# Three layer normalisations taken into the batch loops, and an edge gather that comes before its projection

## The chip, the cores and the metric

The kernel runs on one core of a Trainium2 chip, in float32 but for one stage. The metric is the device time of one launch, in microseconds.

## The reference, cut to what matters

`x` is 16 batches of 512 rows and 128 features, `adj` a 512 x 512 matrix. Four graph layers follow each other, each as `x = layernorm(x + layer(x))` over the 128 features of a row: (0) eight Euler steps, (1) attention over all nodes, (2) a filter in the eigenbasis of the graph's Laplacian, (3) attention along 256 edges `src -> dst`. The diff touches the normalisations behind layers 1, 2 and 3 and the first half of layer 3:

```python
def _layernorm(x, axis=-1, eps=1e-05):
    m = jnp.mean(x, axis=axis, keepdims=True)
    v = jnp.var(x, axis=axis, keepdims=True)
    return (x - m) / jnp.sqrt(v + eps)
# layer 2, U the eigenvectors
agg = jnp.einsum('mn,bnd->bmd', U.T, features)
h = jax.nn.relu(agg @ W1 + b1)
return jnp.einsum('nm,bmd->bnd', U, h @ W2 + b2)
# layer 3, 4 heads
Xq = (H @ W_lin.T).reshape(bt, n, h, dh)
Xv = (H @ W_val.T).reshape(bt, n, h, dh)
Qs, Kt = Xq[:, src], Xq[:, dst]
e = jnp.einsum('behd,hd->beh', jax.nn.leaky_relu(Qs + Kt, LRELU_SLOPE), a)
e = e + jnp.log(A0[src, dst] + EPS)[None, :, None]
# softmax over the edges of one src, then
Y = jax.ops.segment_sum(attn[..., None] * Xv[:, dst], src, num_segments=n)
return Y @ W_out.T
```

## The kernel before, in words

The program is a row of stages, each a block in which every engine has its own list of instructions and waits on semaphores; a stage begins when all engines have left the one before. The Laplacian, its tridiagonal form, its eigenvectors and layer 0 take the first 3390 us or so; then come `attend` (layer 1), `filter_spectrum` (layer 2) and `edge_attend` (layer 3). The whole of `x` stays in SBUF as `m.x`, 128 partitions x 16 batches x 4 chunks x 128 features.

`Norm` normalises all 16 batches at once. VectorE takes the statistics of 64 chunks (L1356), forms mean and variance of all rows in seven small operations (L1358 to L1364), ScalarE takes the square root (L1379), VectorE the reciprocal, and then both scale the chunks, VectorE 40 (L1369) and ScalarE 24 (L1382). It stands behind the batch loops of `attend`, `filter_spectrum` and `edge_attend`, and once ahead of `attend`.

`filter_spectrum` runs over the batches. ScalarE copies a batch into `xs` (`stage`, L1618). TensorE's turn b is: `aggregate` of batch b+1 (L1584), the hidden layer of b (L1601), `spread` of b-1 (L1592), the output `op` of b (L1607). VectorE adds the bias into `o` when `op` is ready (L1646) and then adds `spread`'s result to `x` (L1641, `finish`).

`edge_attend` has a set-up on VectorE (L1835 to L1850: one-hot matrices of `src` and `dst`), a product that picks rows of `adj` (`picked`, L1720), and then two loops over the batches. Loop A: GpSimd copies a batch into `xs` (L1698, L1701), TensorE transposes it (L1727), projects it to queries and values (L1734) and gathers the rows of both ends by one-hots, with 16 matmuls of 128 columns (L1746, L1749); ScalarE moves the results in between (L1803, L1808); VectorE takes two copies from PSUM and forms the scores (L1862 to L1868). Softmax over edges follows for all batches at once. Loop B: VectorE weights the values into `msg` (L1894), TensorE scatters them (L1787) and projects them (L1780) with a copy by ScalarE in between (L1826), VectorE adds the result to `x` (L1904, `finish`). VectorE's order is message b, then `finish` of b-1; TensorE's is scatter b, then projection of b-1. After the last `Norm`, SP issues 16 stores (L1709).

The loops are `batches(...)`: two batches written out, then a loop instruction over pairs, then the last ones written out. A matmul in float32 shows as two passes in the trace, so that "x8" is four matmuls.

Of the kernel before, what the change touches and what calls it, by code (L numbers as in the profile page):

```python
# [1403 lines left out]
def attend(nc, m):  # L1404


    with ExitStack() as ctx:
# [63 lines left out]
        def _(act):  # L1471
# [28 lines left out]
            norm.scalar(act)  # L1500

        @block.vector
        def _(dve):
# [56 lines left out]
            norm.vector(dve)  # L1560


def filter_spectrum(nc, m):

    with ExitStack() as ctx:  # L1565
        (staged, agg_ready, agg_taken, hid_ready, hid_taken, o_ready, o_taken, y_ready, y_taken) = sems(
            nc, ctx, "f_staged f_agg_ready f_agg_taken f_hid_ready f_hid_taken f_o_ready f_o_taken f_y_ready f_y_taken")
        sb = lambda n, *s: ctx.enter_context(nc.sbuf_tensor("f_" + n, [P, *s], F32))
        xs, agg, hid, o = sb("xs", 2, C, F), sb("agg", 2, N), sb("hid", N), sb("o", 2, C, F)
# [4 lines left out]
        norm = Norm(nc, ctx, m, "f_norm")  # L1574
        block = ctx.enter_context(nc.Block())
        whole = lambda b: m.x[:, b] if isinstance(b, int) else m.x[:, bass.ds(b, 1), :, :].rearrange("p o c f -> p (o c) f")

        @block.tensor
        def _(pe):
            def aggregate(b, u):  # L1580
                pe.wait_ge(staged, b + 1)
                after(pe, agg_taken, b - 1)
                for c in range(C):
                    t = nc.tensor.matmul(aggp[:, u, :], xs[:, u, c, :], m.U[:, c, :], start=(c == 0), stop=(c == C - 1))  # L1584
                t.then_inc(agg_ready, 1)

            def spread(b, u):
                pe.wait_ge(o_taken, b + 1)
                after(pe, y_taken, b - 1)
                for r in range(C):  # L1590
                    for c in range(C):
                        t = nc.tensor.matmul(yp[:, u, r, :], m.UT[:, c, r * P:(r + 1) * P], o[:, u, c, :], start=(c == 0),  # L1592
                                             stop=(c == C - 1))
                t.then_inc(y_ready, 1)

            def batch(b, u):
                if not isinstance(b, int) or b < B - 1:
                    aggregate(b + 1, 1 - u)
                pe.wait_ge(agg_taken, b + 1)
                after(pe, hid_taken, b)  # L1600
                nc.tensor.matmul(hidp[:], m.w["L2_gnn_W1"][:], agg[:, u, :], start=True, stop=True).then_inc(hid_ready, 1)  # L1601
                if not isinstance(b, int) or b > 0:
                    spread(b - 1, 1 - u)
# [5 lines left out]

            aggregate(0, 0)  # L1610
            batches(pe, batch, B - 1)
            spread(B - 1, (B - 1) % 2)

        @block.scalar
        def _(act):
            def stage(b, u):
                after(act, agg_ready, b - 1)
                nc.scalar.activation(xs[:, u], whole(b), ACT.Copy).then_inc(staged, 1)  # L1618

            def batch(b, u):  # L1620
                if not isinstance(b, int) or b < B - 1:
                    stage(b + 1, 1 - u)
                act.wait_ge(agg_ready, b + 1)
                after(act, hid_ready, b - 1)
                nc.scalar.activation(agg[:, u, :], aggp[:, u, :], ACT.Copy).then_inc(agg_taken, 1)
# [3 lines left out]

            stage(0, 0)  # L1630
            batches(act, batch, B - 1)
            norm.scalar(act)

        @block.vector
        def _(dve):
# [3 lines left out]
            def finish(b, u):  # L1639
                dve.wait_ge(y_ready, b + 1)  # L1640
                v.tensor_tensor(whole(b), whole(b), yp[:, u], ALU.add).then_inc(y_taken, 1)  # L1641

            def batch(b, u):
# [3 lines left out]
                if not isinstance(b, int) or b > 0:  # L1647
                    finish(b - 1, 1 - u)

            batches(dve, batch, B - 1)  # L1650
            finish(B - 1, (B - 1) % 2)
            dve.wait_ge(y_taken, B)
            norm.vector(dve)
# [8 lines left out]
def edge_attend(nc, m, out):  # L1662

    with ExitStack() as ctx:
        (step, prep, prep_taken, picked, log_go, log_done, ready, staged, xT_ready, xT_taken, qv_ready, qv_taken, gath_ready,
         gath_taken, eT_ready, eT_taken, erow_ready, erow_taken, exp_go, exp_done, den_ready, msg_ready, yT_ready,
         yT_taken, y_ready, y_taken, stored) = sems(
            nc, ctx, "e_step e_prep e_prep_taken e_picked e_log_go e_log_done e_ready e_staged e_xT_ready e_xT_taken e_qv_ready "
                     "e_qv_taken e_gath_ready e_gath_taken e_eT_ready e_eT_taken e_erow_ready e_erow_taken e_exp_go "
                     "e_exp_done e_den_ready e_msg_ready e_yT_ready e_yT_taken e_y_ready e_y_taken e_stored")  # L1670
        sb = lambda n, *s: ctx.enter_context(nc.sbuf_tensor("e_" + n, [P, *s], F32))
        src_of, dst_of, both = sb("src_of", C, E), sb("dst_of", C, E), sb("both", C, E)
# [4 lines left out]
        loga, xs, xT = sb("loga", Q), sb("xs", C, F), sb("xT", N)  # L1677
        qv = sb("qv", 2, C, 2 * F)
# [17 lines left out]
        @block.gpsimd  # L1696
        def _(pool):
            nc.gpsimd.tensor_copy(xs[:], m.x[:, 0]).then_inc(staged, 1)  # L1698
            with pool.Fori(1, B) as b:
                pool.wait_ge(xT_ready, b)  # L1700
                nc.gpsimd.tensor_copy(xs[:], m.x[:, bass.ds(b, 1), :, :].rearrange("p o c f -> p (o c) f")).then_inc(staged, 1)  # L1701

        @block.sync
        def _(sp):
            sp.wait_ge(norm.dve_part, 1)
# [7 lines left out]
        def _(pe):  # L1713
# [10 lines left out]
            def transpose(b):  # L1724
                pe.wait_ge(staged, b + 1)
                for c in range(C):
                    t = nc.tensor.transpose(tp[:, c, :], xs[:, c, :], m.ident[:])  # L1727
                t.then_inc(xT_ready, 1)

            def project(b):  # L1730
                pe.wait_ge(xT_taken, b + 1)
                after(pe, qv_taken, b)
                for c in range(C):
                    t = nc.tensor.matmul(qvp[:, c, :], xT[:, c * P:(c + 1) * P], wqv[:], start=True, stop=True)  # L1734
                t.then_inc(qv_ready, 1)

            def gather(b, u):
                if not isinstance(b, int) or b < B - 1:
                    project(b + 1)
                if not isinstance(b, int) or b < B - 2:  # L1740
                    transpose(b + 2)
                pe.wait_ge(qv_taken, b + 1)
                after(pe, gath_taken, b)
                for q in range(Q):
                    for c in range(C):
                        nc.tensor.matmul(gp[:, q, 0:F], both[:, c, q * P:(q + 1) * P], qv[:, u, c, 0:F], start=(c == 0),  # L1746
                                         stop=(c == C - 1))
# [48 lines left out]
        def _(act):  # L1796
# [3 lines left out]
            def take_xT(b):  # L1800
                act.wait_ge(xT_ready, b + 1)
                after(act, qv_ready, b)
                nc.scalar.activation(xT[:].rearrange("p (c n) -> p c n", c=C), tp[:], ACT.Copy).then_inc(xT_taken, 1)  # L1803

            def take_qv(b, u):
# [189 lines left out]
```

## Time and profile before

| | us |
|---|---|
| three runs | 4143.9, 4145.84, 4145.85; median 4145.84 |
| profiled execution | 4153.18 |
| its span, first to last instruction | 4151.4 |
| from the last sum of layer 1 to the end of the span | 492 |

Over the span TensorE is busy for 69%, VectorE for 76%, ScalarE for 21%, GpSimd for 29%; TensorE's granted clock is 0.65 of full speed in the mean. These shares are those of the long first part; each stage behind it has its own. "Granted clock" is 0.5 (1.2 GHz) or 1.0 (2.4 GHz) at any time, and what lies between is a mean over a stretch. In the timeline a row is a run of equal instructions: its start, its length, engine, line, operation, output and inputs, count, and in brackets the idle time ahead of it and who ended that. The end of a matmul is modelled and lies somewhat behind the start of what follows it.

### The profile page before, as it was taken

To read this page: it belongs to the slowest core of one execution; us is meant where nothing else is said; L and a number is where in the kernel's file an instruction comes from. 1 tells how busy PE (TensorE), PEld (TensorE's weight loads), DVE (VectorE), ACT (ScalarE), POOL (GpSimd) and SP (SyncE) were. 2 spreads that over 40 slices of the span, in tenths; PEclk is the share of its full clock that TensorE was granted. 3 is DMA by queue.
4 is the path that set the end of the run, shared out by engine and by line. 5 is a ranking of instruction groups with operands and counts; after the bars stand their busy time and mean duration, and the time that the engine had idled before them with its cause. 6 is when DMAs were issued, how large, how long until landed. Compare 5 with 4: busy or idle time off the path is not lost. (4 is left out here: it accounts for less than half of the span.)

```text
span 4151.4 us, 77402 instructions
## 1 busy us (share of the span) xinstructions
PE 2843.8 (69%) x21043; PEld 2136.5 (51%) x21043; DVE 3157.0 (76%) x18105; ACT 864.7 (21%) x3720; POOL 1218.4 (29%) x5211
## 2 busy tenths in 40 slices
PE   4778778777776666665558667748496446769694
PEld 3666666666654545444448434425353225646662
DVE  4888888888888888888873788899999548942463
ACT  1212222222223333333320001001010002321201
POOL 1554555555555555555550111000000000000000
PEclk8555555555555555555555778879798668889868
DMA  1000000000000000000011000000000000000001
GB/s 59 2 2 2 2 2 2 2 2 2 2 2 2 1 2 1 1 1 1 1 55 32 1 1 1 1 1 0 0 1 0 0 0 0 0 0 0 0 1 41
DMA packets 23019, 23.83 MB, mean 6 GB/s; under 512 B 3024, under 2 KB 21328, under 8 KB 22096
## 3 DMA queue, kind: packets, MB, share of 16 engines
q1 hardware_dynamic: 22608, 19.17, 1.4%
q8 instruction: 158, 2.59, 0.3%
q14 instruction: 253, 2.07, 0.2%
HBM read 14.97 MB, written 4.19 MB: 5 GB/s over the span
## 5 line engine op out<-in xcount | busy, mean ns | idle before, releaser
L373 PE MATMUL h_sums<-h_P,ones 128*128 128x60 f32 (+3 forms) x1020 | 315.3, 404 | 244.3 <-DVE h_P L559 165.8
L831 PE MATMUL d_acc<-d_h,U 128*128 128x512 f32 x1024 | 471.4, 604 | 0.0
L381 PE MATMUL h_axp<-h_XV,ident 128*128 128x64 f32 x1018 | 337.2, 435 | 184.4 <-POOL h_XV L425 184.4
L354 PE MATMUL h_sums<-h_parts,ones 128*128 128x19 f32 (+2 forms) x1020 | 315.5, 399 | 188.0 <-DVE h_parts L512 163.0
L373 PEld LDWEIGHTS h_sums<-h_P,ones 128*128 128x128 f32 x1020 | 255.0, 310 | 304.9 <-issue 304.9
L362 PE MATMUL h_axp<-h_XV,x 128*128 128x4 bf16 x11514 | 388.5, 169 | 17.0 <-DVE h_CX L523 16.5
L354 PEld LDWEIGHTS h_sums<-h_parts,ones 128*128 128x128 f32 x1020 | 256.7, 312 | 273.9 <-DVE h_parts L512 234.1
L381 PEld LDWEIGHTS h_axp<-h_XV,ident 128*128 128x128 f32 x1018 | 254.4, 310 | 267.4 <-DVE h_y L597 218.3
L411 POOL TENSOR_TENSOR h_root<-urow,h_halves 128x1 f32<-128x1 f32 x510 | 278.1, 545 | 380.2 <-DVE urow L564 380.2
L362 PEld LDWEIGHTS h_axp<-h_XV,x 128*128 128x128 bf16 x11514 | 362.6, 105 | 33.9 <-DVE h_CX L523 25.4
L831 PEld LDWEIGHTS d_acc<-d_h,U 128*128 128x128 f32 x1024 | 188.8, 195 | 202.2 <-issue 202.2
L432 ACT ACTIVATE h_ntau<-h_EE 128x1 f32<-128x1 f32 x510 | 101.5, 199 | 845.9 <-DVE h_EE L595 835.3
L472 ACT ACTIVATE h_XV<-h_XV,urow 128x1 f32<-128x1 f32 x382 | 133.7, 382 | 567.0 <-DVE urow L577 567.0
L882 POOL TENSOR_TENSOR m_c_mid<-m_c_m,m_halves 128x4 f32<-128x4 f32 x53 | 53.4, 1008 | 545.1 <-DVE m_c_m L1135 545.1
L1105 DVE RECIPROCAL m_work<-m_work 128x512 f32<-128x512 f32 (+8 forms) x53 | 206.3, 3892 | 0.0
L844 ACT ACTIVATE d_h<-d_acc 128x512 f32<-128x512 f32 x128 | 76.5, 598 | 535.7 <-PE d_acc L831 524.6
L821 PEld LDWEIGHTS d_acc<-G,d_xT 128*128 128x128 f32 x1152 | 156.4, 201 | 59.6 <-issue 55.5
L1698 POOL COPY e_xs<-x 128x512 f32<-128x512 f32 x1 | 0.6, 611 | 630.0 <-POOLq L1565 630.0
L564 DVE COPY urow<-h_sums 128x2 f32<-128x2 f32 x510 | 80.8, 159 | 125.4 <-PE h_sums L354 123.9
L401 POOL TENSOR_TENSOR h_XV<-h_XV 128x4 f32<-128x4 f32 (+3 forms) x510 | 101.0, 198 | 227.3 <-DVE h_XV L621 183.3
L600 DVE SCALAR_TENSOR_TENSOR h_zp<-h_y,h_EE,below 128x4 f32<-128x4 f32 (+3 forms) x510 | 125.7, 247 | 53.5 <-DVE h_y L597 0.5
L821 PE MATMUL d_acc<-G,d_xT 128*128 128x128 f32 x1152 | 158.7, 286 | 3.1 <-ACT d_xT L844 3.1
(566 smaller groups left out, 6975.9 us busy)
## 6 DMA issues: line engine op xcount, KB each, us to landing
cut<-in_c_cut SPq DMA_DIRECT2D x1, 4608.0 KB, 14.0
x<-in_x SPq DMA_DIRECT2D x16, 256.0 KB, 4.3
out<-x SPq DMA_DIRECT2D x16, 256.0 KB, 3.6
adj<-in_adj SPq DMA_DIRECT2D x1, 1024.0 KB, 5.2
below<-in_c_below SPq DMA_DIRECT2D x1, 1024.0 KB, 7.3
neps<-in_c_neps SPq DMA_DIRECT2D x1, 1024.0 KB, 8.4
UT<-in_c_ramp SPq DMA_DIRECT2D x1, 1024.0 KB, 10.3
same<-in_c_same SPq DMA_DIRECT2D x1, 448.0 KB, 9.9
```

Of the source, the lines that this page charges most:

```text
L354: nc.tensor.matmul(PS1[:, lo:hi], m.ones[:], parts[:, lo:hi], start=True, stop=True).then_inc(sums_ready, 1)
L362: t = nc.tensor.matmul(AX4[:, r, :], part[:, c, r * P:(r + 1) * P], XVb[:, c, 2 * XS + 1::68], start=(c == c0 and i == 0), stop=(c == C - ...
L373: nc.tensor.matmul(PS2[:, :, T1 * c0:], m.ones[:], P2[:, :, c0:, :].rearrange("p i c t -> p i (c t)"), start=True, stop=True).then_inc(pv_ ...
L381: nc.tensor.matmul(sides(PSE), m.ident[:, r:r + 1].broadcast_to([P, P]), sides(XV[:, cr, 0:2 * RIGHT]), start=True, stop=True).then_inc(ro ...
L401: do(g.tensor_tensor(XV[:, c0:, RS], XV[:, c0:, XS], XVb[:, c0:, 2 * XS + 1], ALU.subtract))
L411: g.tensor_tensor(root[:], TT[:, k, 4:5], halves[:], ALU.pow).then_inc(root_done, 1)
L432: copy = lambda out, in_, **k: nc.scalar.activation(out, in_, ACT.Copy, **k)
L472: t = nc.scalar.activation(XV[:, c, vslot(k):vslot(k) + 1], XV[:, c, ES:ES + 1], ACT.Identity, scale=TT[:, k, 3:4], bias=XV[:, c, XS:XS + 1])
L600: zp_done = do.send(v.scalar_tensor_tensor(zp[:, c0:C], y[:, c0:C], EE[:, k, 3:4], column(m.below, k + 1)[:, c0:C], ALU.mult, ALU.mult))
L821: i = nc.tensor.matmul(acc[:, j, :], self.xT[:, r, j, :], m.G[:, k, :], start=(j == 0), stop=(k == T_STEPS), skip_group_check=True)
L831: i = nc.tensor.matmul(acc, m.mixT[:, c, r * P:(r + 1) * P], src[:, :, c, :], start=False, stop=(c == C - 1), skip_group_check=True)
L1105: do(v.reciprocal(part(work), part(work)))
```

## The change

`Norm` is replaced by `RowNorm`, which works on one batch: `moments(b)` on VectorE, a power of -1/2 on GpSimd (`root`), `scale(b)` on VectorE. The normalisation behind layer 1 moves to `filter_spectrum`: batches 0 and 1 ahead of its loop, batch b+2 in turn b. That behind layer 2 moves to `edge_attend`: batches 0, 1 and 2 ahead of the set-up, batch b+3 in turn b of loop A. That behind layer 3 (`close`) goes into loop B: `moments` directly behind the sum of a batch, `scale` two messages later, and each batch's store waits for its own scale. The normalisation ahead of `attend` stays as it was.

The matmuls read `m.x` in place of a staged copy. In loop A the rows of `x` are gathered first: four matmuls of 512 columns by `pick`, which holds the 256 columns of `src` + `dst` beside the 256 of `dst`, one copy by ScalarE, and then four projections of 128 columns. The batch loops of the filter, of loop A and of VectorE's part of loop B are written out in full.

```diff
+class RowNorm:
+    def moments(self, dve, b):
+        v, st = self.nc.vector, self.stats
+        mean, diff, var = (self.col[:, b % 2, i, :] for i in range(3))
+        do = Steps(dve, self.step, b * 3)
+        for c in range(C):
+            t = v.bn_stats(st[:, c, :], self.m.x[:, b, c, :])
+        do(t)
+        v.tensor_tensor(mean, st[:, :, 1], st[:, :, 4], ALU.add)
+        v.tensor_tensor(diff, st[:, :, 1], st[:, :, 4], ALU.subtract)
+        do(v.tensor_tensor(var, st[:, :, 2], st[:, :, 5], ALU.add))
+        v.tensor_scalar(mean, mean, 0.5, None, ALU.mult)
+        v.tensor_scalar(var, var, 1.0 / F, 1e-5, ALU.mult, ALU.add)
+        do(v.tensor_tensor(diff, diff, diff, ALU.mult))
+        v.scalar_tensor_tensor(var, diff, 0.25, var, ALU.mult, ALU.add).then_inc(self.var_ready, 1)
+    def root(self, pool):
+        for b in range(B):
+            pool.wait_ge(self.var_ready, b + 1)
+            self.nc.gpsimd.tensor_tensor(self.col[:, b % 2, 3, :], self.col[:, b % 2, 2, :], self.minus_half[:],
+                                         ALU.pow).then_inc(self.root_done, 1)
+    def scale(self, dve, b):
+        mean, rstd = self.col[:, b % 2, 0, :], self.col[:, b % 2, 3, :]
+        dve.wait_ge(self.root_done, b + 1)
+        for c in range(C):
+            x = self.m.x[:, b, c, :]
+            t = self.nc.vector.tensor_scalar(x, x, mean[:, c:c + 1], rstd[:, c:c + 1], ALU.subtract, ALU.mult)
+        t.then_inc(self.normed, 1)
...
 def filter_spectrum(nc, m):
...
-            def aggregate(b, u):
-                pe.wait_ge(staged, b + 1)
+            def aggregate(b):
+                pe.wait_ge(norm.normed, b + 1)
                 after(pe, agg_taken, b - 1)
                 for c in range(C):
-                    t = nc.tensor.matmul(aggp[:, u, :], xs[:, u, c, :], m.U[:, c, :], start=(c == 0), stop=(c == C - 1))
+                    t = nc.tensor.matmul(aggp[:, b % 2, :], m.x[:, b, c, :], m.U[:, c, :], start=(c == 0), stop=(c == C - 1))
...
+            norm.begin()
+            for b in range(2):
+                norm.moments(dve, b)
+                norm.scale(dve, b)
+            for b in range(B):
+                if b + 2 < B:
+                    norm.moments(dve, b + 2)
                 dve.wait_ge(o_ready, b + 1)
                 after(dve, y_ready, b - 1)
-                v.tensor_tensor(o[:, u], op[:], bias, ALU.add).then_inc(o_taken, 1)
-                if not isinstance(b, int) or b > 0:
-                    finish(b - 1, 1 - u)
+                v.tensor_tensor(o[:, b % 2], op[:], bias, ALU.add).then_inc(o_taken, 1)
+                if b + 2 < B:
+                    norm.scale(dve, b + 2)
+                if b:
+                    finish(b - 1)
...
 def edge_attend(nc, m, out):
...
             for b in range(B):
-                if b * C == norm.SPLIT:
-                    sp.wait_ge(norm.act_part, 1)
+                sp.wait_ge(close.normed, b + 1)
                 sp.dma_start(out[b].rearrange("(c p) f -> p c f", p=P), m.x[:, b]).then_inc(stored, 16)
...
+            def gather(b):
+                pe.wait_ge(norm.normed, b + 1)
+                after(pe, xg_taken, b - 1)
+                for c in range(C):
+                    t = nc.tensor.matmul(xgp[:, b % 2, :], m.x[:, b, c, :], pick[:, c, :], start=(c == 0), stop=(c == C - 1))
+                t.then_inc(xg_ready, 1)
             def project(b):
-                pe.wait_ge(xT_taken, b + 1)
-                after(pe, qv_taken, b)
+                pe.wait_ge(xg_taken, b + 1)
                 after(pe, gath_taken, b)
+                for a in range(2):
+                    for q in range(Q):
+                        t = nc.tensor.matmul(gp[:, q, a * F:(a + 1) * F], xg[:, b % 2, a * E + q * P:a * E + (q + 1) * P],
+                                             wqv[:, a * F:(a + 1) * F], start=True, stop=True)
                 t.then_inc(gath_ready, 1)
-            transpose(0)
-            project(0)
-            transpose(1)
-            batches(pe, gather, B - 1)
+            gather(0)
+            for b in range(B):
+                if b < B - 1:
+                    gather(b + 1)
+                project(b)
...
+            for b in range(3):
+                norm.moments(dve, b)
+                norm.scale(dve, b)
             v.tensor_copy(rowf[:], m.edge_row[:])
...
-            with dve.Fori(0, B) as b:
+            for b in range(B):
                 lp = Steps(dve, step, b * PER_A + base)
+                if b + 3 < B:
+                    norm.moments(dve, b + 3)
                 dve.wait_ge(gath_ready, b + 1)
                 v.tensor_copy(t1[:], gp[:, :, 0:F])
...
                 lp(v.tensor_tensor(t2[:], t2[:], m.w["L3_gnn_a"][:].unsqueeze(1).broadcast_to([P, Q, F]), ALU.mult))
+                if b + 3 < B:
+                    norm.scale(dve, b + 3)
...
             def finish(b):
                 dve.wait_ge(y_ready, b + 1)
-                v.tensor_tensor(x, x, yp[:], ALU.add).then_inc(y_taken, 1)
+                v.tensor_tensor(m.x[:, b], m.x[:, b], yp[:], ALU.add).then_inc(y_taken, 1)
+                dve.wait_ge(y_taken, b + 1)
+                close.moments(dve, b)
+            for b in range(B):
+                message(b)
+                if b > 1:
+                    close.scale(dve, b - 2)
+                if b:
+                    finish(b - 1)
+            close.scale(dve, B - 2)
             finish(B - 1)
-            dve.wait_ge(y_taken, B)
-            norm.vector(dve)
+            close.scale(dve, B - 1)
```

## Rows read from the trace of the kernel before

**Rows 1.** Windows: stretch, length, busy us (count) of five engines, clock, DMA.
```profile
3692.00:3831.00 139.00, 137.06 (x792) 99.95 (x790) 20.31 (x32) 25.84 (x46) 0.00 (x0) 1.00 0.00 0
...
3879.00:3980.00 101.00, 94.24 (x704) 88.77 (x702) 34.22 (x87) 25.68 (x34) 9.25 (x15) 0.98 0.00 0
...
4044.00:4112.00 68.00, 47.70 (x192) 28.27 (x192) 17.20 (x35) 10.84 (x17) 0.00 (x0) 0.97 0.00 0
```

**Rows 2.** Timeline, end of the filter loop.
```profile
3820.33 1.02 PE L1601 MATMUL f_hid_ps<-f_agg,w_L_gnn_W 128*128 128x512 f32 x2
3820.53 0.69 DVE L1646 TENSOR_TENSOR f_o<-f_o_ps,w_L_gnn_b 128x512 f32<-128x512 f32 x1 [7.47 <-PE f_o_ps L1607]
3821.14 0.68 DVE L1641 TENSOR_TENSOR x<-x,f_y_ps 128x512 f32<-128x512 f32 x1
...
3821.28 3.84 PE L1592 MATMUL f_y_ps<-f_o,UT 128*128 128x128 f32 x32
```

**Rows 3.** Timeline, the normalisation behind layer 1 and the filter's start.
```profile
3659.20 12.47 DVE L1356 BATCH_NORM_STATS2 a_norm_stats<-x 128x6 f32<-128x128 f32 x64
...
3674.12 10.34 DVE L1369 TENSOR_SCALAR x<-x,a_norm_col 128x128 f32<-128x128 f32 x40
...
3684.97 1.15 ACT L1618 ACTIVATE f_xs<-x 128x512 f32<-128x512 f32 x2 [1.39 <-PEq L1407]
...
3685.65 9.43 PE L1584 MATMUL f_agg_ps<-U,f_xs 128*128 128x512 f32 x16 [27.87 <-ACT f_xs L1618]
```

**Rows 4.** Timeline of VectorE in an earlier stage, operations on 128x4.
```profile
2276.10 0.15 DVE L1133 TENSOR_TENSOR m_c_b<-m_c_v,m_c_F 128x4 f32<-128x4 f32 x1
2276.17 0.16 DVE L1134 TENSOR_TENSOR m_c_a<-m_c_v,m_c_a 128x4 f32<-128x4 f32 x1
2276.36 0.17 DVE L1135 TENSOR_TENSOR m_c_m<-m_c_lo,m_c_hi 128x4 f32<-128x4 f32 x1
```

**Rows 5.** Timeline, first stage: VectorE behind GpSimd's power on 128x4.
```profile
41.09 0.16 DVE L202 TENSOR_TENSOR deg<-deg 128x4 f32<-128x4 f32 x1 [1.13 <-POOL deg L175]
```

**Rows 6.** Timeline, the picked rows of `adj`.
```profile
3869.10 9.86 PE L1720 MATMUL e_rp<-adj,e_src_of 128*128 128x512 f32 x16 [11.06 <-DVE e_woT L1850]
```

**Rows 7.** Timeline of VectorE in loop A: first turn, second turn, last turn.
```profile
3892.58 0.42 DVE L1862 COPY e_t<-e_gp 128x256 f32<-128x256 f32 x1 [12.07 <-PE e_gp L1749]
...
3898.32 0.42 DVE L1862 COPY e_t<-e_gp 128x256 f32<-128x256 f32 x1 [3.50 <-PE e_gp L1749]
...
3900.14 0.42 DVE L1868 TENSOR_REDUCE e_ee<-e_t 128x256 f32 x1
...
3977.24 0.42 DVE L1862 COPY e_t<-e_gp 128x256 f32<-128x256 f32 x1 [2.51 <-PE e_gp L1749]
```

**Rows 8.** Timeline of TensorE: `attend`, and loop A's first two projections.
```profile
3598.15 5.50 PE L1462 MATMUL a_out<-a_wh,a_pr 128*128 128x131 f32 x32 [3.24 <-ACT a_pr L1495]
...
3881.28 3.65 PE L1734 MATMUL e_qvp<-e_wqv,e_xT 128*128 128x256 f32 x8 [1.89 <-ACT e_xT L1803]
...
3886.54 1.99 PE L1734 MATMUL e_qvp<-e_wqv,e_xT 128*128 128x256 f32 x8 [1.14 <-ACT e_xT L1803]
```

**Rows 9.** Timeline of loop B: its first sum, and one turn near the end.
```profile
4051.52 0.69 DVE L1904 TENSOR_TENSOR x<-x,e_yp 128x512 f32<-128x512 f32 x1 [6.10 <-PE e_yp L1780]
...
4105.14 0.69 DVE L1904 TENSOR_TENSOR x<-x,e_yp 128x512 f32<-128x512 f32 x1 [2.97 <-PE e_yp L1780]
4105.74 0.42 DVE L1894 TENSOR_TENSOR e_msg<-e_vt,e_den 128x256 f32<-128x256 f32 x1
...
4106.22 1.98 PE L1787 MATMUL e_rp<-e_src_to,e_msg 128*128 128x512 f32 x4 [1.11 <-DVE e_msg L1894]
...
4108.04 1.05 PE L1780 MATMUL e_yp<-e_woT,e_yT 128*128 128x128 f32 x8
...
4109.13 0.69 DVE L1904 TENSOR_TENSOR x<-x,e_yp 128x512 f32<-128x512 f32 x1 [2.97 <-PE e_yp L1780]
```

**Rows 10.** Timeline, the stores at the end.
```profile
4137.13 10.17 SPq L1709 DMA_DIRECT2D out<-x  x16
```

More of the change, by code:

```diff
@@ L1559, in _, with __init__, begin @@
             dve.wait_ge(out_taken, B)
-            norm.vector(dve)
+class RowNorm:
+    def __init__(self, nc, ctx, m, name):
+        self.nc, self.m = nc, m
+        self.step, self.var_ready, self.root_done, self.normed = sems(
+            nc, ctx, " ".join(name + n for n in ("_step", "_var_ready", "_root_done", "_normed")))
+        sb = lambda n, *s: ctx.enter_context(nc.sbuf_tensor(name + n, [P, *s], F32))
+        self.stats, self.col, self.minus_half = sb("_stats", C, 6), sb("_col", 2, 5, C), sb("_minus_half", C)
+    def begin(self):
+        self.nc.vector.memset(self.minus_half[:], -0.5)
+    def moments(self, dve, b):
[24 more added lines that the diff above has]
+        t.then_inc(self.normed, 1)
@@ L1608, in batch @@
                 t.then_inc(o_ready, 1)
-            aggregate(0, 0)
-            batches(pe, batch, B - 1)
-            spread(B - 1, (B - 1) % 2)
+            spread(B - 1)
         @block.scalar
         def _(act):
[L1616 to L1622, printed above, removed]
+            for b in range(B):
                 act.wait_ge(agg_ready, b + 1)
                 after(act, hid_ready, b - 1)
-                nc.scalar.activation(agg[:, u, :], aggp[:, u, :], ACT.Copy).then_inc(agg_taken, 1)
+                nc.scalar.activation(agg[:, b % 2, :], aggp[:, b % 2, :], ACT.Copy).then_inc(agg_taken, 1)
                 act.wait_ge(hid_ready, b + 1)
@@ L1798, in _ @@
             nc.scalar.activation(loga[:], loga[:], ACT.Ln).then_inc(log_done, 1)
[L1800 to L1805, printed above, removed]
-                act.wait_ge(qv_ready, b + 1)
-                after(act, gath_ready, b - 1)
-                nc.scalar.activation(qv[:, u], qvp[:], ACT.Copy).then_inc(qv_taken, 1)
-            def batch(b, u):
-                if not isinstance(b, int) or b < B - 1:
-                    take_qv(b + 1, 1 - u)
-                if not isinstance(b, int) or b < B - 2:
-                    take_xT(b + 2)
-            take_xT(0)
-            take_qv(0, 0)
-            take_xT(1)
-            batches(act, batch, B - 1)
+            for b in range(B):
+                act.wait_ge(xg_ready, b + 1)
+                after(act, gath_ready, b - 1)
+                nc.scalar.activation(xg[:, b % 2, :], xgp[:, b % 2, :], ACT.Copy).then_inc(xg_taken, 1)
             act.wait_ge(exp_go, 1)
@@ L1834, in _ @@
             do = Steps(dve, step)
+            norm.begin()
+            close.begin()
+            for b in range(3):
+                norm.moments(dve, b)
+                norm.scale(dve, b)
             v.tensor_copy(rowf[:], m.edge_row[:])
```

107 lines of the change are left out of this document (37 added, 70 removed).

## The prediction

> **What bounds the kernel now.** I read the run times first, then the page, then the table of stages, then the timeline of each stage that the diff touches, and last the pace of TensorE behind idle stretches. Everything up to the end of `attend` is untouched, so only the last 490 us count. In them three things set the time.
>
> The filter loop is TensorE's: 137.06 us busy of 139 at a granted clock of 1.00, while VectorE works for 20.31 [rows 1]. Edge loop A (`gather`) is TensorE's as well, 94.24 of 101, with VectorE at 34.22 [rows 1]. Edge loop B (`scatter`, `project_out`) is a ring: VectorE adds batch b-1 into x, only then writes message b+1, TensorE scatters it and projects, VectorE waits again. One turn in straight-line code is 4105.14 to 4109.13, 3.99 us: 0.60 to the message, 0.48 to TensorE's start, 2.91 on TensorE; the mean over 14 turns is (4109.13 - 4051.52)/14 = 4.115 [rows 9]. Between the loops stand three whole-tensor normalisations with TensorE idle: from 3659.20 to the next stage's first instruction at 3684.97 is 25.8 us [rows 3], the second is like it, and behind the third come 16 stores in a row [rows 10].
>
> **Prices of one batch's normalisation.** The four statistics issue at 12.47/64 = 0.195 us each [rows 3], with the landing that the next step waits for 0.89. Of the seven small operations on 128x4, independent ones follow at 0.07, one that waits for the last at 0.19 [rows 4]: two groups of three at 0.34 and a last at 0.08. `moments` is then 0.89 + 0.68 + 0.08 = 1.65. GpSimd's power on the same shape returns 1.13 after VectorE's last result [rows 5], that is 1.21 after `moments` has issued. `scale` is 4 x 10.34/40 = 1.03, and lands 0.07 later [rows 3]. A normalisation with nothing beside it: 3.9.
>
> **Filter, head.** Before, TensorE's first aggregate starts at 3685.65, 26.45 after the statistics begin [rows 3]. After: change of stage 0.5 (3674.12 + 10.34 to 3684.97, rows 3), a memset 0.1, one normalisation 3.9, landing and start 0.13: 4.6. Gain 21.8. Batch 1's normalisation lies under aggregate 0. ScalarE's staging copy goes too, but it lay under matmuls: nothing.
>
> **Filter, loop.** Here the order costs. `scale(b+2)` stands on VectorE behind `o` of batch b, which waits for `o_ready(b)`, TensorE's last work of its turn b. TensorE's first work of turn b+1 is aggregate b+2, which now waits for that scale. Everything of the next turn is queued behind it. The wait: VectorE starts `o` 0.20 after TensorE would have gone on (3820.33 to 3820.53), 0.61 to the next instruction, `scale` with landing 1.10, 0.06 to TensorE, 0.1 for the first weights: 2.07 [rows 2, 3]. The last is read from loop B, where four passes of 512 columns behind a wait are followed after 1.82 (4106.22 to 4108.04), though a pass takes 0.43: two are recorded with 1.02, of which 0.16 is the modelled end, by which the four's 1.98 overruns too [rows 2, 9]. Aggregates 0 and 1 are prepared ahead, 2 to 15 wait: 14 x 2.07 = 29.0. `moments` and the power cost nothing here, VectorE is idle for 118 of 139 us [rows 1]. Filter in sum: +7.2.
>
> **Edge, head.** 25.8 of normalisation and stage change become 0.5 + 0.2 + 3 x 3.9 = 12.4 ahead of an unchanged set-up: gain 13.4. `picked` still ends where it did, TensorE free at about 3878.8 [rows 6]. Then 13.8 us passed to the first result at 3892.58 [rows 7]. Now: two gathers of 8 passes of 512 columns, 3.44 each, 6.9 together [rows 2], and a projection of 8 passes of 128 columns, 1.05 [rows 9]: 8.0. Gain 5.8.
>
> **Edge loop A.** TensorE goes from 5.74 (3892.58 to 3898.32, rows 7) to 3.44 + 0.89 = 4.33 per batch; the projection's 1.05 without its modelled end is 0.89. VectorE had 2.24 (3898.32 to 3900.14, and 0.42) [rows 7] and gets `moments` and `scale`: 2.24 + 1.65 + 1.03 = 4.92, and becomes the bound. The power's 1.21 is hidden behind the copies and the two operations after them, 1.8. Twelve turns at 4.92, and then the last three batches: 2.9 to the last scale, 3.44, 1.05, 0.8 for the two copies, 1.05, in sum 9.2. That is 68.2 for 84.66 now (3892.58 to 3977.24): gain 16.4. Bounds: 65 if TensorE alone counts (15 x 4.33), 84.7 if every VectorE step is a quarter dearer (6.3 a turn). GpSimd's and ScalarE's copies go; they lay under matmuls.
>
> **Edge loop B.** `close.moments` comes between the sum and the next message, on the ring, with the sum's landing: 0.72 + 1.65 + 0.48 + 2.91 = 5.76. `close.scale(b-2)` follows the message and lies under TensorE's 2.91 (its power is back 1.2 after `moments`, it ends at 2.2). 14 x (5.76 - 4.115) = +23.0.
>
> **Tail.** From the next-to-last sum to the end is 4151.4 - 4109.13 = 42.3 now. After: sum, moments, power, scale, twice over, 0.72 + 1.65 + 1.21 + 1.03 = 4.6 and 4.7, one store issued in 10.17/16 = 0.64, and the 4.1 that the last landing and the end take now (4147.30 to 4151.4) [rows 10]: 14.0. Gain 28.3. The other stores go out during the loop; SP has nothing else queued.
>
> Loops become straight-line code: nothing, since the unrolled turn of rows 9 is not slower than the mean. Sum so far: +7.2 - 13.4 - 5.8 - 16.4 + 23.0 - 28.3 = -33.7.
>
> **The clock.** Idle stretches on TensorE cost a second time. Loop A's first projection, behind an idle 1.89, took 3.65 us; the next, the same eight passes, 1.99. The first ran at half the pace, the lower level of 1.2 GHz, which cost 1.66. In `attend` an idle 3.24 stands ahead of 32 passes that take 5.50, where 8 take 1.05, so at full pace 3.7: 1.8 lost [rows 8, 9]. Loop B's idle of 1.1 per turn left the granted clock at 0.97 over the stage [rows 1]. In loop B the idle becomes 0.72 + 1.65 + 0.48 = 2.9: nearer to 3.24 than to 1.1, and above the 1.89 that fell once. I take 12 falls in 14 turns at 1.66: +20. Bounds: nothing, and 14 x 2.6 = 36 if TensorE's passes of a turn, 1.72 + 0.89, all stay at 1.2 GHz. The filter's idle is 1.8, beside the 1.89; it stands between long matmuls, and I take two or three falls in 14, +4, bounds 0 and 14 x 1.66 = 23.
>
> Sum: -33.7 + 20 + 4 = -9.7. The profiled execution took 4153.18 (span 4151.4), so 4143.5; it stands 7.3 above the median of the runs, 4145.84, so the forecast is **4136**.
>
> **Rivals.**
> - *The clock holds in both loops.* The 0.97 of loop B speaks for it, the fall behind 1.89 against. Time: 4145.8 - 33.7 = 4112. The Trainium skill, "TensorE: Matmul & The Clock Gate", section "Why this matters for your kernels", asks for idle gaps between bursts of matmuls to be kept short, and this gap is just shorter than the length that it names; by that rule the clock would hold and the time be 4112. The trace does not agree with it: the fall behind 1.89 in rows 8.
> - *The clock falls at every added wait* and loop B never leaves 1.2 GHz: +36 there, +23 in the filter, -33.7 + 59 = +25, 4171, slower. Against it: in `attend` the clock comes back within each batch. It decides from 42 us of clock cost on (33.7 + 8.3).
> - *Loop A gains nothing*, because VectorE, with GpSimd beside it, needs 6.3 per turn instead of 4.9: -9.7 + 16.4 = +7, 4153, no change that can be told. For it: VectorE issues 20 instructions a turn for 5. Against: each is priced from a row of its own.
>
> **How the numbers follow.** Forecast 0.62, its own range 4126 to 4147 (6 to 14 falls in loop B, 0 to 5 in the filter, moments off by 0.1 in 28 turns); clock holds 0.17; clock falls everywhere 0.10; loop A without gain 0.11. The range takes in the clock that holds, with 3 us for its prices, and leaves out the clock that falls everywhere and half of the loop-A case, 0.16 in sum: 4109 to 4152. Changes under 0.2%, 8.3 us, are about what a measurement of this kernel can't tell from none. Faster than that: 0.37 of the forecast's 0.62 (it lies only 1.4 beyond the line), all 0.17, and 0.01 of the loop-A case: 0.55. Slower: 0.08 of the clock case, 0.03 of the loop-A case, 0.01 of the forecast's: 0.12. Same: 0.33.
>
> **What would show it.** Filter: TensorE idle about 1.8 ahead of 14 of 16 aggregates, released by VectorE's scale; each turn 2.07 longer. Loop A: VectorE without idle, turns of 4.9. Loop B: turns of 5.8 at full clock, mean above 7, granted clock around 0.75 instead of 0.97. Tail of 14. The prediction is wrong if loop B's granted clock stays near 1.00 (then 20 us better), or falls in the filter at each wait, or if loop A's turn is 4.3 (VectorE's steps overlap more than priced) or 5.7.

## The result and the profile after

The changed kernel takes 4140.57 us, the median of 12 runs (4132.78 to 4142.13), beside 4147.99 (4143.9 to 4153.48) of 12 runs of the kernel before. Between the medians that is 7.4 us less; the ratio estimated from all these runs is 0.9977, 95% interval 0.9968 to 0.9985, that is 0.23% less. The forecast was 4136.

The two profiled executions differ by more than that, 4132.87 against 4153.18. About half of this lies in the untouched part, which took unequal times: `attend`'s last sum starts at 3658.04 before and at 3648.39 after. So the stages are compared from there on, 493.4 us before (to 4151.4) and 482.5 after (to 4130.9): -10.9.

| Stretch, us | before | after | difference | predicted |
|---|---|---|---|---|
| last sum of `attend` to last sum of the filter | 172.6 | 182.1 | +9.5 | +11 |
| to the first result of loop A | 61.9 | 41.0 | -21.0 | -19.2 |
| loop A, first to last result | 84.7 | 68.0 | -16.7 | -16.4 |
| to the first sum of loop B (not changed) | 74.3 | 74.3 | 0.1 | 0 |
| loop B, 14 turns | 57.6 | 105.1 | +47.5 | +43 |
| tail | 42.3 | 12.0 | -30.3 | -28.3 |

The windows of the profile after, in the columns of [rows 1]: filter, loop A, loop B, tail.

```profile
3654.10:3831.00 176.90, 149.51 (x800) 104.57 (x800) 59.31 (x257) 18.91 (x32) 15.10 (x15) 0.97 0.00 1
3856.00:3936.00 80.00, 77.45 (x256) 40.86 (x255) 63.55 (x270) 9.16 (x16) 13.09 (x13) 0.99 0.00 1
4005.50:4117.00 111.50, 69.09 (x175) 37.89 (x176) 54.53 (x242) 8.96 (x15) 15.71 (x14) 0.73 0.10 31
4117.00:4131.00 14.00, 3.00 (x18) 2.17 (x16) 6.82 (x32) 0.60 (x1) 2.01 (x2) 0.74 0.19 56
```

In the filter TensorE is no longer busy throughout: 149.5 of 176.9, where [rows 1] had 137 of 139. In loop B the granted clock is 0.73 where it was 0.97, and TensorE's busy time grew although a turn has the same 12 passes. The 0.97 was the start of the stage alone: in the 14 turns from 4051.52 to 4109.13 the clock before was 1.00 throughout.

Filter, timeline, the head and one turn of the loop:

```profile
3650.06 0.29 DVE L1579 BATCH_NORM_STATS2 f_norm_stats<-x 128x6 f32<-128x128 f32 x1 [0.55 <-PEq L1407]
...
3654.11 1.22 PE L1628 MATMUL f_agg_ps<-U,x 128*128 128x512 f32 x1 [5.98 <-DVE x L1600]
...
3698.46 1.06 PE L1652 MATMUL f_o_ps<-w_L_gnn_W,f_hid 128*128 128x128 f32 x8
3699.56 0.69 DVE L1684 TENSOR_TENSOR f_o<-f_o_ps,w_L_gnn_b 128x512 f32<-128x512 f32 x1 [6.86 <-PE f_o_ps L1652]
3700.17 1.11 DVE L1600 TENSOR_SCALAR x<-x,f_norm_col 128x128 f32<-128x128 f32 x4
...
3701.33 3.70 PE L1628 MATMUL f_agg_ps<-U,x 128*128 128x512 f32 x8 [1.81 <-DVE x L1600]
...
3710.39 0.69 DVE L1684 TENSOR_TENSOR f_o<-f_o_ps,w_L_gnn_b 128x512 f32<-128x512 f32 x1 [6.85 <-PE f_o_ps L1652]
```

The first aggregate starts 4.05 us behind the first statistics, for 26.45 in [rows 3]. In the loop TensorE ends the passes for `o`, VectorE adds the bias, scales the batch after next, and only then TensorE starts its aggregate, after 1.81 idle. A turn is 10.83 (3699.56 to 3710.39). The waits of TensorE in the filter's stretch, summed by what ended them (us, times, longest):

```profile
PE f_agg_ps L1628 <- DVE x L1600: 31.3, 15, 6.0
```

That is the first aggregate's 6.0 and 14 more of 1.81.

Loop A, timeline of VectorE: first two turns, and the last.

```profile
3871.47 0.42 DVE L1873 COPY e_t<-e_gp 128x256 f32<-128x256 f32 x1 [4.22 <-PE e_gp L1769]
...
3873.18 1.12 DVE L1600 TENSOR_SCALAR x<-x,e_norm_col 128x128 f32<-128x128 f32 x4
3874.21 0.41 DVE L1880 TENSOR_REDUCE e_ee<-e_t 128x8 f32<-128x256 f32 x1
3874.66 0.87 DVE L1579 BATCH_NORM_STATS2 e_norm_stats<-x 128x6 f32<-128x128 f32 x4
...
3876.33 0.42 DVE L1873 COPY e_t<-e_gp 128x256 f32<-128x256 f32 x1
...
3939.47 0.42 DVE L1873 COPY e_t<-e_gp 128x256 f32<-128x256 f32 x1
```

Against [rows 7], the copy of the second turn has no idle time ahead of it: VectorE's own work fills the turn of 4.86 us, and TensorE waits for it.

Loop B, timeline: one turn from sum to sum, TensorE's passes of the next two, and the sums that end them.

```profile
4013.82 0.69 DVE L1913 TENSOR_TENSOR x<-x,e_yp 128x512 f32<-128x512 f32 x1 [6.82 <-PE e_yp L1801]
4014.54 0.87 DVE L1579 BATCH_NORM_STATS2 e_close_stats<-x 128x6 f32<-128x128 f32 x4
...
4016.22 0.42 DVE L1906 TENSOR_TENSOR e_msg<-e_vt,e_den 128x256 f32<-128x256 f32 x1
...
4016.77 1.98 PE L1808 MATMUL e_rp<-e_src_to,e_msg 128*128 128x512 f32 x4 [2.99 <-DVE e_msg L1906]
...
4019.68 0.69 DVE L1913 TENSOR_TENSOR x<-x,e_yp 128x512 f32<-128x512 f32 x1 [1.03 <-PE e_yp L1801]
...
4022.55 3.38 PE L1808 MATMUL e_rp<-e_src_to,e_msg 128*128 128x512 f32 x4 [2.91 <-DVE e_msg L1906]
...
4026.85 0.69 DVE L1913 TENSOR_TENSOR x<-x,e_yp 128x512 f32<-128x512 f32 x1 [2.34 <-PE e_yp L1801]
...
4029.80 3.78 PE L1808 MATMUL e_rp<-e_src_to,e_msg 128*128 128x512 f32 x4 [2.99 <-DVE e_msg L1906]
...
4035.32 0.69 DVE L1913 TENSOR_TENSOR x<-x,e_yp 128x512 f32<-128x512 f32 x1 [3.64 <-PE e_yp L1801]
...
4118.91 0.69 DVE L1913 TENSOR_TENSOR x<-x,e_yp 128x512 f32<-128x512 f32 x1 [2.45 <-PE e_yp L1801]
```

The first turn is the one of [rows 9] with the statistics and small operations set between sum and message: 5.86. The same four scatter passes take 1.98 there, then 3.38 and 3.78, and the turns 7.17 and 8.47: the lower level of the clock, for all or a part of a turn. Windows that are nearly these three turns show it in the granted clock, the last but two of the columns:

```profile
4013.00:4019.70 6.70, 3.65 (x20) 2.32 (x18) 3.81 (x18) 1.12 (x2) 1.12 (x1) 1.00 0.01 4
4019.70:4026.90 7.20, 4.27 (x12) 2.28 (x12) 3.82 (x18) 0.60 (x1) 1.12 (x1) 0.76 0.23 70
4026.90:4034.00 7.10, 4.20 (x7) 2.14 (x8) 3.74 (x17) 0.30 (x1) 1.12 (x1) 0.63 0.12 37
```

The other 11 turns take 7.21 to 8.47, so the first alone ran at full clock. The mean of the 14 turns is (4118.91 - 4013.82)/14 = 7.51. In the first experiment below, whose loop B is the same, they take 106.5 instead of 105.1, again one of 5.86 and 13 above 7.3.

The tail, timeline: the last scale; the span ends at 4130.9.

```profile
4127.13 1.11 DVE L1600 TENSOR_SCALAR x<-x,e_close_col 128x128 f32<-128x128 f32 x4 [1.12 <-POOL e_close_col L1592]
```

### The profile page after: what moved, and what is told of

Its sections match the earlier page's. It is cut to its first block and busy times, and to the rows that moved or that the text cites. A ratio compares the mean times of both kernels' runs of the same rounds, so it can differ in the third digit from the quotient of the medians.

```text
span 4130.9 us, 76408 instructions
## 1 busy us (share of the span) xinstructions
PE 2841.4 (69%) x20595; PEld 2094.8 (51%) x20595; DVE 3209.4 (78%) x18489; ACT 810.3 (20%) x3611; POOL 1252.0 (30%) x5243
## 3 DMA queue, kind: packets, MB, share of 16 engines
q14 instruction: 255, 2.09, 0.2%
## 5 line engine op out<-in xcount | busy, mean ns | idle before, releaser
L1592 POOL TENSOR_TENSOR f_norm_col<-f_norm_col,f_norm_minus_half 128x4 f32<-128x4 f32 x16 | 16.1, 1007 | 564.0 <-DVE f_norm_col L1587 564.0
L425 POOL TENSOR_TENSOR h_XV<-h_sa,h_y 128x4 f32<-128x4 f32 (+3 forms) x510 | 99.7, 196 | 202.0 <-DVE h_y L597 202.0
## 6 DMA issues: line engine op xcount, KB each, us to landing
UT<-in_c_ramp SPq DMA_DIRECT2D x1, 1024.0 KB, 10.5
```

## The experiments

The theory: the change gains at both heads, in loop A and in the tail what its parts were priced at, and gives some 79 us back by two orders on VectorE, the filter's scale behind `o` and the closing moments ahead of the next message; about half of the second loss is TensorE's clock. Each run is given as its ratio to runs of the kernel before on the same chip (the changed kernel: 0.9977).

**The filter's scale ahead of o**, from the changed kernel:

```diff
                 if b + 2 < B:
                     norm.moments(dve, b + 2)
+                    norm.scale(dve, b + 2)
                 dve.wait_ge(o_ready, b + 1)
                 after(dve, y_ready, b - 1)
                 v.tensor_tensor(o[:, b % 2], op[:], bias, ALU.add).then_inc(o_taken, 1)
-                if b + 2 < B:
-                    norm.scale(dve, b + 2)
```

> The changed kernel, but in the filter loop the scale of batch b+2 stands ahead of the wait for o of batch b, right behind its moments. If the order alone makes TensorE wait (theory), the idle of 1.81 us ahead of 14 aggregates, released by VectorE's scale, is gone, the filter's turn goes from 10.83 to 8.76 us and the stage loses 14 x 2.08 = 29 us: about 4112 for the median of 4140.6. VectorE now stands 1.2 us for GpSimd's power in each turn, which it has to spare. Rival: TensorE is held by something else as well (the arrays that VectorE and TensorE share, or o arriving late because VectorE stands at the power), and under 10 us come back.

Measured: 4106.04 for 4151.13, ratio 0.9894 (0.9879 to 0.9909). The window of the loop, the one wait that is left, and a turn of its timeline:

```profile
3656.50:3802.00 145.50, 143.84 (x800) 102.87 (x800) 60.17 (x257) 18.88 (x32) 15.10 (x15) 0.98 0.00 1
```

```profile
PE f_agg_ps L1628 <- DVE x L1600: 6.0, 1, 6.0
```

```profile
3704.38 3.60 PE L1628 MATMUL f_agg_ps<-U,x 128*128 128x512 f32 x8
3704.58 0.69 DVE L1685 TENSOR_TENSOR f_o<-f_o_ps,w_L_gnn_b 128x512 f32<-128x512 f32 x1 [3.57 <-PE f_o_ps L1652]
...
3708.65 1.12 DVE L1600 TENSOR_SCALAR x<-x,f_norm_col 128x128 f32<-128x128 f32 x4 [1.12 <-POOL f_norm_col L1592]
...
3713.34 0.69 DVE L1685 TENSOR_TENSOR f_o<-f_o_ps,w_L_gnn_b 128x512 f32<-128x512 f32 x1 [3.57 <-PE f_o_ps L1652]
```

TensorE starts the aggregate ahead of `o`, VectorE stands 1.12 us for GpSimd inside time that it has, and the stage (3650.87 to 3802.30) is 151.4 for 182.1: -30.7, of which 14 x 2.07 = 29.0 is the wait, a turn of 8.76 (3704.58 to 3713.34) for 10.83. The other 1.7 is the one turn of the changed kernel in which the clock fell, which took 12.53. The order was the whole loss.

**The message ahead of the closing moments**, from the changed kernel; `finish` is left with the sum alone:

```diff
+            def moments(b):
+                dve.wait_ge(y_taken, b + 1)
+                close.moments(dve, b)
             for b in range(B):
                 message(b)
-                if b > 1:
-                    close.scale(dve, b - 2)
+                if b > 2:
+                    close.scale(dve, b - 3)
+                if b > 1:
+                    moments(b - 2)
                 if b:
                     finish(b - 1)
-            close.scale(dve, B - 2)
+            close.scale(dve, B - 3)
+            moments(B - 2)
             finish(B - 1)
+            close.scale(dve, B - 2)
+            moments(B - 1)
             close.scale(dve, B - 1)
```

> The changed kernel, but in loop B the closing moments of a batch come one turn later, behind the next message and the scale of the batch before it, so that they lie under TensorE's scatter and projection. Theory (the moments' place costs 1.65 us of wait and the clock falls on top): the turn goes from a mean of 7.51 back to about 4.1, the granted clock of the loop from 0.73 to 0.97 or more, the loop loses 47 us; the tail has two moments and three scales behind the next-to-last sum instead of two and two, 1 to 2 us more: about 4095. Rival (VectorE's added 2.7 us a turn cost whatever their place, with GpSimd beside it): a turn of 5.8 to 6.8, 4106 to 4120.

Measured: 4091.23 for 4151.13, ratio 0.9853 (0.9838 to 0.9868). The 14 turns as a window, and a turn of the timeline:

```profile
4022.98:4079.27 56.29, 40.22 (x168) 24.19 (x168) 49.51 (x235) 8.36 (x14) 13.30 (x14) 1.00 0.20 61
```

```profile
4039.08 0.69 DVE L1913 TENSOR_TENSOR x<-x,e_yp 128x512 f32<-128x512 f32 x1 [0.27 <-PE e_yp L1801]
4039.69 0.42 DVE L1906 TENSOR_TENSOR e_msg<-e_vt,e_den 128x256 f32<-128x256 f32 x1
4040.02 1.11 DVE L1600 TENSOR_SCALAR x<-x,e_close_col 128x128 f32<-128x128 f32 x4
4040.24 1.98 PE L1808 MATMUL e_rp<-e_src_to,e_msg 128*128 128x512 f32 x4 [1.20 <-DVE e_msg L1906]
...
4041.05 0.86 DVE L1579 BATCH_NORM_STATS2 e_close_stats<-x 128x6 f32<-128x128 f32 x4
...
4043.15 0.69 DVE L1913 TENSOR_TENSOR x<-x,e_yp 128x512 f32<-128x512 f32 x1 [0.35 <-PE e_yp L1801]
```

Scale and moments lie under TensorE's passes with 0.3 us to spare, TensorE's idle time is back to 1.2, the clock to 1.00 and the turn to 4.02. VectorE does 49.5 us of work in the stretch, 3.5 a turn, and it costs nothing: the place was the price. The tail is 12.3.

**TensorE kept busy in the wait**, from the changed kernel: work that nobody reads is added behind each projection of loop B.

```diff
                     project_out(b - 1, 1 - u)
+                    for _ in range(5):
+                        nc.tensor.matmul(xgp[:, 0, :], src_of[:, 0, 0:P], pick[:, 0, :], start=True, stop=True)
```

> The changed kernel with work added: in loop B TensorE runs five matmuls of 512 columns, whose result nobody reads, behind each projection, while VectorE adds, takes the moments and writes the next message. They take 2.2 us at full pace of a wait of 2.9. The order of the kernel's own work and every wait stay. Theory (the clock falls cost 20 of the loop's 47.5 us, the wait itself the rest): granted clock near 1.00, a turn of 5.8 to 5.9 instead of 7.51, 14 turns 82 instead of 105: 4117. Rival (the clock costs nothing that ends up in the time, and the 7.51 is made of dearer VectorE and GpSimd work): turn and time as before, 4141, or later by what the added matmuls delay.

Measured: 4130.75 for 4151.13, ratio 0.9953 (0.994 to 0.9967). The 14 turns as a window:

```profile
4019.04:4115.70 96.66, 96.66 (x309) 49.75 (x308) 53.12 (x239) 8.36 (x14) 15.70 (x14) 1.00 0.13 38
```

The expectation took a matmul of 512 columns for one pass. It is two, 0.86 us, so the five take 4.3 us where the wait was 2.9, and TensorE, never idle, sets a turn of 6.90. The run shows that the clock then stays at 1.00, and that the loop was 8.4 us shorter with 4.3 us of work for nothing in every turn than without. It does not give the price of the clock. So the same again with less:

```diff
                     project_out(b - 1, 1 - u)
+                    for n in (2 * E, 2 * E, E):
+                        nc.tensor.matmul(xgp[:, 0, 0:n], src_of[:, 0, 0:P], pick[:, 0, 0:n], start=True, stop=True)
```

> The busy wait of loop B again, with less work in it. A matmul of 512 columns takes 0.86 us, two of the passes that the prediction counted, so that the five took 4.3 us of a wait of 2.9 and set the turn themselves. Now two of 512 and one of 256 columns, 2.15 us at full pace. Theory (the fall of the clock is a cost of its own, 1.65 a turn): granted clock near 1.00 in the loop, the turn 5.86 as in the changed kernel's one warm turn, 14 turns 82 for 105, the run 23 below the changed kernel: about 4118. Rival (the turn is long because of VectorE and GpSimd): 7.5 a turn whatever TensorE does in the wait, 4141.

Measured: 4118.03 for 4150.89, ratio 0.9924 (0.991 to 0.9938). The 14 turns as a window, and one in the timeline:

```profile
4021.90:4103.40 81.50, 70.41 (x254) 38.00 (x253) 53.14 (x239) 8.36 (x14) 15.70 (x14) 1.00 0.14 42
```

```profile
4027.61 2.31 PE L1813 MATMUL e_xgp<-e_pick,e_src_of 128*128 128x512 f32 x6
4027.81 0.69 DVE L1915 TENSOR_TENSOR x<-x,e_yp 128x512 f32<-128x512 f32 x1 [1.03 <-PE e_yp L1801]
...
4030.21 0.42 DVE L1908 TENSOR_TENSOR e_msg<-e_vt,e_den 128x256 f32<-128x256 f32 x1
```

From the sum to the message it is 2.40 us, as in the changed kernel (4013.82 to 4016.22), and VectorE's time in the 14 turns is the same too (53.1). The turn is (4103.37 - 4021.95)/14 = 5.82 for 7.51, and close to the 5.86 of the changed kernel's one turn at full clock, which had no added work. Loop B's 47.5 us over the kernel before are then 14 x (5.82 - 4.115) = 23.9 of wait and 14 x (7.51 - 5.82) = 23.7 of clock. The rival, dear VectorE and GpSimd work, is out.

**The closing normalisation undone**: whole again behind loop B, the stores behind it; the rest as changed.

```diff
-        norm, close = RowNorm(nc, ctx, m, "e_norm"), RowNorm(nc, ctx, m, "e_close")
+        norm, close = RowNorm(nc, ctx, m, "e_norm"), Norm(nc, ctx, m, "e_close")
...
-                dve.wait_ge(y_taken, b + 1)
-                close.moments(dve, b)
...
             for b in range(B):
                 message(b)
-                if b > 1:
-                    close.scale(dve, b - 2)
                 if b:
                     finish(b - 1)
-            close.scale(dve, B - 2)
             finish(B - 1)
-            close.scale(dve, B - 1)
+            dve.wait_ge(y_taken, B)
+            close.vector(dve)
```

> One part undone: the closing normalisation is again that of the kernel before, whole, behind loop B, and the stores behind it; the filter, the edge head and loop A stay changed. By the changed kernel's trace the closing part costs 47.5 us in the loop and gives 30.3 in the tail (12.0 for 42.3), so undoing it should make the kernel faster by 17: about 4123. If the loop's turn was long for another reason (unrolled code, the new loop A's leftovers), it stays above 5 us and the time goes up by the tail's 30 instead: about 4170.

Measured: 4122.92 for 4151.13, ratio 0.9929 (0.9915 to 0.9942), about 20 us better than the whole change. The 14 turns as a window:

```profile
4022.56:4078.89 56.33, 40.22 (x168) 24.19 (x168) 14.34 (x29) 8.64 (x15) 0.00 (x0) 1.00 0.00 0
```

The turn is 4.02 in straight-line code without moments, and the tail 42.2 (4078.89 to the span's end at 4121.1). As it was written, the closing part lost 48.8 and gained 30.2: by itself it made the kernel slower.

**The new gather alone**, in the kernel before, with the three whole normalisations left (x is normalised ahead of the stage, so `gather` waits for none):

```diff
-            def transpose(b):
...
-            def gather(b, u):
...
+            def gather(b):
+                after(pe, xg_taken, b - 1)
+                for c in range(C):
+                    t = nc.tensor.matmul(xgp[:, b % 2, :], m.x[:, b, c, :], pick[:, c, :], start=(c == 0), stop=(c == C - 1))
+                t.then_inc(xg_ready, 1)
...
```

> One part done alone: the kernel before with nothing but the new gather (one-hots of 512 columns, then the projection) in loop A; the three whole normalisations, the filter and loop B are as before. Theory (loop A was TensorE's, and the new order of products is worth 5.74 - 4.33 us a turn): TensorE sets a turn of 4.33, first to last result 65 for 84.66, and the first result 5.8 earlier: 25 us less than the kernel before, where the whole change gained 10. VectorE, with 2.2 us of work in a turn, has idle time. In the changed kernel the turn was 4.85 with VectorE without idle, so the normalisations would cost 0.5 a turn there, 6 us in 12. Rival (the gather was worth nothing by itself, since the copies of ScalarE between the two products hold TensorE): a turn of 5 to 5.7, less than 12 us gained.

Measured: 4118.62 for 4150.89, ratio 0.9929 (0.9916 to 0.9943). Loop A as a window, and two turns in VectorE's timeline:

```profile
3881.81:3945.01 63.20, 61.67 (x232) 34.54 (x230) 30.39 (x75) 9.66 (x15) 0.00 (x0) 1.00 0.00 1
```

```profile
3881.81 0.42 DVE L1826 COPY e_t<-e_gp 128x256 f32<-128x256 f32 x1 [6.25 <-PE e_gp L1728]
...
3886.14 0.42 DVE L1826 COPY e_t<-e_gp 128x256 f32<-128x256 f32 x1 [2.09 <-PE e_gp L1728]
```

TensorE sets the turn at 4.33, VectorE idles 2.09 in it; loop A is 63.2 for 84.7 and the first result comes 56.0 behind the filter's last sum (3825.81) instead of 61.9. This one part is worth about 29 us by the ratio and 27 by the stages (466.4 from `attend`'s last sum on, for 493.4), more than the whole change. With the normalisations in the loop VectorE binds at 4.86, 0.53 more in each of 12 turns: 6 us.

**Both orders together**: the diffs of the first two runs.

> The changed kernel with both reorderings, the filter's scale ahead of o and the closing moments behind the next message. If the two losses are separate stages, the gains add: by the traces 30.7 in the filter (181.7 to 151.0 from the last sum of attend to the last of the filter) and 48.8 - 0.3 in loop B and the tail, 79 together: about 0.979 of the kernel before, 4062 where the changed kernel is at 4141. If they share a cause (the clock's course from one stage into the next), less: above 4070.

Measured: 4056.73 for 4150.89, ratio 0.9782 (0.9768 to 0.9796). From `attend`'s last sum on it takes 403.4 for 482.5, 79.1 less, where the two runs alone gave 30.7 in the filter, 48.8 in the loop and -0.3 in the tail, 79.2 in sum: the two losses were separate.

**A version that beats both**: the two orders; the first two normalisations of the edge stage behind the set-up, under the 8.77 us that VectorE waited for the picking; and loop A's copy of the values on ScalarE.

```diff
-            for b in range(3):
-                norm.moments(dve, b)
-                norm.scale(dve, b)
             v.tensor_copy(rowf[:], m.edge_row[:])
...
             v.tensor_copy(woT[:], tp[:, 2, :]).then_inc(prep_taken, 1)
+            for b in range(2):
+                norm.moments(dve, b)
+                norm.scale(dve, b)
             dve.wait_ge(picked, 1)
...
             v.tensor_scalar(loga[:], loga[:], 1e-8, None, ALU.add).then_inc(log_go, 1)
+            norm.moments(dve, 2)
+            norm.scale(dve, 2)
             dve.wait_ge(log_done, 1)
...
-                v.tensor_copy(t1[:], gp[:, :, 0:F])
-                v.tensor_copy(vt[:, b], gp[:, :, F:2 * F]).then_inc(gath_taken, 1)
+                v.tensor_copy(t1[:], gp[:, :, 0:F]).then_inc(gath_taken, 1)
...
+            def take_vt(b):
+                act.wait_ge(gath_taken, b + 1)
+                nc.scalar.activation(vt[:, b], gp[:, :, F:2 * F], ACT.Copy).then_inc(vt_taken, 1)
```

> A version meant to beat both kernels: the two reorderings, and in the edge stage the first two normalisations behind the set-up, where VectorE waited 8.77 us for TensorE's picking, the third behind the sum of the picking; and in loop A the copy of the values on ScalarE instead of VectorE. Head: the set-up begins 11.7 us earlier and the first result with it, about -11.7. Loop A: VectorE's turn loses a copy of 0.35 us but now waits for the landing of the one that stays, 4.85 to 4.5 to 4.6, 12 x 0.3 = -3.6 (against 4.33 that TensorE needs). With the 79 of the two reorderings -94: about 4047 where the changed kernel is at 4141. If VectorE is late with the third batch's scale in the new head, TensorE stands behind its second gather and the head gives 4 us less.

Measured: 4046.26 for 4150.89, ratio 0.9749 (0.9735 to 0.9762). Loop A as a window, and VectorE's first turn:

```profile
3834.92:3898.71 63.79, 62.59 (x232) 34.90 (x230) 57.52 (x244) 14.13 (x29) 12.48 (x13) 1.00 0.00 1
```

```profile
3834.92 0.42 DVE L1882 COPY e_t<-e_gp 128x256 f32<-128x256 f32 x1 [0.69 <-PE e_gp L1769]
...
3839.45 0.42 DVE L1882 COPY e_t<-e_gp 128x256 f32<-128x256 f32 x1
```

The first result comes 29.2 behind the filter's last sum (3805.68) for 41.0 in the changed kernel: -11.7. The turn is 4.53 for 4.86, loop A 63.8 for 68.0: -4.2. The two edits are 15.9 by the stages, 10.5 between the medians of this run and the last; the intervals allow either.

## Why the prediction was right

The mechanism and the size held: -10.9 by the stages where the sum was -9.7, and -7.4 between the medians. The forecast of 4136 lies 4.4 below the median: 2.2 because the kernel before has a median of 4147.99 in 12 runs where three gave 4145.84, and 2.3 because the medians differ by 7.4 and not by 9.7.

That the sum is off by only 1.2 by the stages is in part luck. Loop B cost 4.5 more than predicted; the filter, the edge head, loop A and the tail together came out 5.8 better. And the largest uncertain term, 12 falls of the clock in loop B, was a choice between bounds of 0 and 36 us, not the result of a sum. By its steps:

- **Filter, head**: 4.6 predicted, 4.59 measured from the end of `attend`'s last sum to the first aggregate.
- **Filter, loop**: the wait was 2.07 predicted and 2.07 measured a turn (10.83 against the 8.76 of the first experiment), 14 times, and it was the order alone. Two or three falls of the clock were assumed; the granted clock fell once, for 1.7 us (a turn of 12.53), and in the second experiment, whose filter is the same, not at all. The loop cost +31.4 (first aggregate to last sum, 176.4 for 145.0) where +33 was predicted.
- **Edge, head**: -21.0 for -19.2. The normalisations came as priced (3.9 each, 12.3 to the set-up for 12.4). Two things were not in the sum. The cast that begins the set-up took 0.5 us less (last section). And the picking itself took 8.67 where [rows 6] show 9.86: the granted clock was at the lower level for its first 3.2 us, and for 5.6 before. This varies from run to run: in the second experiment, whose edge head is the same, the picking took 9.51.
- **Loop A**: a turn of 4.86 for 4.92, first to last 68.0 for 68.2. VectorE is the bound, as said; the rival that it gains nothing is out. That rival's turn of 6.3 was called a quarter dearer than 4.92; a quarter more is 6.15, which changes nothing here.
- **Loop B**: the ring at full clock is 5.82 for 5.76, by the shorter busy wait. The clock fell in 13 of 14 turns, for 12 assumed, and a fall cost 23.7/13 = 1.82, for 1.66 from one projection: 23.7 instead of 20. The reading that a wait of 1.1 had cost a little clock before (0.97) was not right, as said above; it had cost none. Some turns run wholly at the lower level (8.47, 2.6 more, the upper bound of the prediction for one turn), others partly (7.17 to 7.55). This is the term that was most off, by 4.5 in sum. The straight-line code was put at nothing; without moments it takes 56.3 us for 57.6 (the run with the closing normalisation undone), a gain of 1.3.
- **Tail**: 12.0 for 14.0. The end behind the last store was taken from 16 stores in a row; one store alone is done 2.7 us after the last scale ends (4128.24 to 4130.9).

The rival that the clock holds in both loops would have needed 5.82 in loop B; the shorter busy wait shows that turn, but only with TensorE given something to do. The rule behind it, in the Trainium skill, "TensorE: Matmul & The Clock Gate", section "Why this matters for your kernels", speaks of keeping idle gaps between bursts short. Here gaps of 2.9 us, shorter than the one that it names, were followed by a fall in 13 of 14 turns, and gaps of 1.2 us in the reordered loop of the second experiment by none.

What the prediction did not say, though its terms held it: which of the parts were worth making. Its sum had the closing part at +43 - 28.3, a loss, and the filter's order at +33 for a head of -21.8, a loss too; the gather and the edge head carried the rest.

## What to carry to other kernels

When normalisation is moved batch by batch into a loop that another engine bounds, and the engine that gets it has the time to spare, its place in that engine's order decides: look for the instruction that the bounding engine waits for next, and put the moved work behind that one. Here the same instructions cost 79 us in one order and next to nothing in the other. Where the time is not there, the length counts as well: in loop A VectorE became the bound, at 0.53 us a turn. A wait in front of TensorE can have two prices, its length and what the clock loses behind it. In loop B they were equal, 23.9 and 23.7 us; in the filter they were 29.0 and 1.7.

## What the runs showed of the hardware

- Adding matmuls for nothing made the kernel faster: 2.15 us of them in each wait of 2.9 took 23.7 us off 14 turns, and even 4.3 us of them, more than the wait, 8.4.
- The first instruction of the edge set-up, the same cast, took half the time after. In the kernel before it starts beside GpSimd's copy of the first batch, which the change took out. The run with the new gather alone separates the two: it begins the stage as the kernel before does, with the same wait of 0.54, but without that copy, and the cast takes 0.43 there. So the copy beside it cost the cast some 0.45 us. Timeline, before and then after:

```profile
3857.16 0.61 POOL L1698 COPY e_xs<-x 128x512 f32<-128x512 f32 x1 [630.05 <-POOLq L1565]
3857.17 0.88 DVE L1835 CAST e_rowf<-edge_row 128x512 f32<-128x512 int32 x1 [0.54 <-PEq L1565]
```

```profile
3843.52 0.42 DVE L1844 CAST e_rowf<-edge_row 128x512 f32<-128x512 int32 x1
```

- The untouched part of the program ends at times that differ by 10 us from one execution to the next (3648.39 and 3658.04 in the two profiles, at the same instruction), as much as the whole effect of this change. Twelve runs of each kernel tell the effect from none; what each part did was to be read only stage by stage, from one instruction to another in each trace.
